# The second attention of a two-layer kernel: the probabilities turned by TensorE, or by VectorE in 32x32 blocks with DMAs that move the blocks

## The chip, the cores and the metric

One NeuronCore of a Trainium2 chip runs the whole program. The metric is the device time of one execution, in microseconds (us). The engines are TensorE (PE in the rows; PEld is its weight load), VectorE (DVE), ScalarE (ACT), GpSimd (POOL) and the sync engine (SP), which here only issues DMAs.

## The reference

Two layers over x of shape (16, 128, 128) and a context of (16, 128, 96), all float32: attention, a mixture of experts, attention, a routed expert network, each added to x. What is changed lies in the second attention, which for each of the 16 batches computes:

```
q_in = x @ Wq + lora                     # 128 tokens, 16 heads of 64
k_in, v_in = first 124 context rows @ Wk, Wv (+ lora)
out = softmax(q k^T / 8) v               # over 124 keys
out_ipa = softmax(q ki^T / 8) vi         # over the last 4 context rows
out = out + out_ipa
x = x + out @ Wo + bo + lora
```

The kernel keeps both softmaxes of a head side by side: 124 + 4 = 128 probabilities for each query. So a batch has a p1 of 128 queries x 16 heads x 128 keys, 1 MB in float32, and the product with the values needs it with the keys on the partitions.

## The kernel before

Each engine has one in-order program written by hand, with semaphores between them. The second attention is a loop of rounds, b = -1 to 16. In round b an engine works on the scores and the softmax of batch b, on the queries, keys and values of batch f = b + 1, on the outputs of batch t = b - 1, and on the first layer's experts of batch g = b + 4 (while g < 16). Z.name are the semaphores of this attention; `after(engine, sem, count)` is a wait that is left out where the count is zero or less.

TensorE's order in round b is: scores(b,0), turn(t,0), queries(f,0), turn(t,1), queries(f,1), ffn(g,0), scores(b,1), turn(t,2), keys(f,0), turn(t,3), ffn(g,1), outputs(t,0), outputs(t,1), keys(f,1), values(f,0), inputs(b+2), values(f,1), and the projection of batch t. A turn is 4 transposes of 128x128 (one head each) through an identity into a PSUM bank; VectorE's turned(t,n) copies the bank to p1T (in the last two batches ScalarE copies two of the four).

VectorE's shifted(b,n) takes the maxima from the scores of 4 heads, ScalarE's powers(b,n) makes the exponentials, VectorE's summed(b,n) the reciprocals, and GpSimd's norm(b,n) (L498) multiplies them in. ipa_norm(b) (L794 to L798) finishes the 4 extra keys of all 16 heads, so a turn needs it too (Z.ipa_p). VectorE ends its round with dve_residual(t), which waits for the projection, and with the statistics and the normalized input of later batches.

SP issues in round f one small DMA (L391, the extra values of batch f), and expert weights: 3 DMAs of 128 KB in rounds 2 to 7, 6 in rounds 13 to 15.

After round 16 comes the routed network, which starts when all outputs of the attention are copied (`pe.wait_ge(Z.o_sb, 2 * B)`).

Of the kernel before, what the change touches and what calls it, by code (L numbers as in the profile page):

```python
# [51 lines left out]
def build_program(nc, T, out):  # L52

    with ExitStack() as ctx:
# [29 lines left out]
        class Arena:  # L84
# [9 lines left out]
            def take(self, shape, dt=F32):  # L94
# [8 lines left out]
                if dt != F32:  # L103
# [151 lines left out]
        Z = named(sem, "z", "xn xb tr xT q q_sb k0 k1 k0_sb k1_sb ki v v_sb vi0 vi1 score ipa_max maxed ipa_exp ipa_step ipa_p "  # L255
                            "exp rsum norm turned p_sb p_odd o o_sb proj x_new stats")

# [13 lines left out]
        FILL = 2  # L271
        LAST_TURNS = B - 2
        SPARE = 14
# [14 lines left out]

        def p_copied(t, n):

            done = CH * min(t, LAST_TURNS) + 2 * max(t - LAST_TURNS, 0) + n + 1
            if t < LAST_TURNS:
                return Z.p_sb, done
            return (Z.p_odd, 2 * (t - LAST_TURNS) + n // 2 + 1) if n % 2 else (Z.p_sb, done - n // 2)

# [61 lines left out]
        def _(sp):  # L357
# [51 lines left out]
        def _(pool):  # L409
# [84 lines left out]
            def norm(b, n):  # L494

                pool.wait_ge(Z.rsum, CH * b + n + 1)
                part = p1[:, b % 2, n, :, 0:ORG]
                pool.tensor_tensor(part, part, rsum1[:, b % 2, CH * n:CH * n + CH].unsqueeze(2).broadcast_to((128, CH, ORG)),  # L498
                                   ALU.mult).then_inc(Z.norm, 1)
# [64 lines left out]
        def _(dve):  # L564
# [226 lines left out]
            def ipa_norm(b):  # L791

                dve.wait_ge(Z.ipa_exp, b + 1)
                dve.tensor_reduce(ipa_sum[:, b % 2, :], ipa_s[:, b % 2, :, :], X, ALU.add).then_inc(Z.ipa_step, 1)  # L794
                dve.wait_ge(Z.ipa_step, b * 2 + 1)
                dve.reciprocal(ipa_sum[:, b % 2, :], ipa_sum[:, b % 2, :]).then_inc(Z.ipa_step, 1)
                dve.wait_ge(Z.ipa_step, b * 2 + 2)
                dve.tensor_tensor(p1[:, b % 2, :, :, ORG:S].rearrange("p n c j -> p (n c) j"), ipa_s[:, b % 2, :, :],  # L798
                                  ipa_sum[:, b % 2, :].unsqueeze(2).broadcast_to((128, H, IPA)), ALU.mult)\
                    .then_inc(Z.ipa_p, 1)  # L800
# [74 lines left out]
            def round1(b):  # L875
                f, t, g = b + 1, b - 1, b + 4
                if there(b):
                    shifted(b, 0)
                if there(t):
                    turned(t, 0)  # L880
# [4 lines left out]
                if there(t):  # L885
                    turned(t, 1)
                if b == 15:
# [19 lines left out]
                if b == 12:  # L907
                    hidden(0)
                if there(t):
                    turned(t, 2)  # L910
                if b == 15:
# [9 lines left out]
                if there(t):  # L921
                    turned(t, 3)
                if b == 13:
# [131 lines left out]
        def _(act):  # L1055
# [89 lines left out]
            def powers(b, n):  # L1145

                act.wait_ge(Z.maxed, CH * b + n + 1)
                for c in range(CH):
                    h = CH * n + c
                    ins = act.activation(p1[:, b % 2, n, c, 0:ORG], blocks(bank[n])[:, c, 0:ORG], ACT.Exp,  # L1150
                                         bias=negmax1[:, b % 2, h:h + 1], accum_out=sums1[:, b % 2, h:h + 1])
# [18 lines left out]
            def turned(t, n):  # L1170

                act.wait_ge(Z.turned, CH * t + n + 1)
                act.activation(p1T[:, CH * n:CH * n + CH, :], blocks(bank[(4, 6, 5, 4)[n]]), ACT.Copy).then_inc(Z.p_odd, 1)

# [28 lines left out]
            def round1(b):  # L1203
# [11 lines left out]
                if there(b):  # L1215
                    powers(b, 1)
                if b == 15:
                    turned(t, 1)
                if there(f):
# [11 lines left out]
                if b == 15:  # L1231
                    turned(t, 3)
                    gathered(1)
                if b == B:
                    gathered(4)
                    turned(t, 1)
                    gathered(5)
                    turned(t, 3)
                if there(b):
# [88 lines left out]
        def _(pe):  # L1328
# [185 lines left out]

            def turn(t, n, freed, count):

                pe.wait_ge(Z.norm, CH * t + n + 1)
                pe.wait_ge(Z.ipa_p, t + 1)
                after(pe, freed, count)
                for c in range(CH):  # L1520
                    mm = pe.transpose(blocks(bank[(4, 6, 5, 4)[n]])[:, c, :], p1[:, t % 2, n, c, :], ident[:, :])  # L1521
                mm.then_inc(Z.turned, 1)

            def queries(f, n, freed, count):
# [16 lines left out]
            def outputs(t, n, freed, count):  # L1541

                for k in (2 * n, 2 * n + 1):
                    pe.wait_ge(*p_copied(t, k))
                pe.wait_ge(Z.v_sb, 2 * t + n + 1)
                pe.wait_ge((Z.vi0, Z.vi1)[t % 2], 16 * (t // 2 + 1))
                after(pe, freed, count)
                for c in range(CH):
                    for odd in range(2):
                        h = 8 * n + 2 * c + odd  # L1550
                        mm = pe.matmul(blocks(bank[5 - n])[D1 * odd:D1 * odd + D1, c, :], v1[:, t % 2, D1 * h:D1 * h + D1],  # L1551
                                       p1T[:, CH * (2 * n + odd) + c, :], start=True, stop=True)
                mm.then_inc(Z.o, 1)
# [58 lines left out]
            def round1(b):  # L1612
# [4 lines left out]
                if there(b):  # L1617
                    scores(b, 0)
                if there(t):
                    turn(t, 0, Z.o_sb, 2 * t)  # L1620
                if b == B:
# [11 lines left out]
                if there(f):  # L1633
                    queries(f, 0, Z.v_sb, 2 * f - 1)
                if there(t):
                    if b == B:
                        pe.wait_ge(G.xg, 4)
                    turn(t, 1, Z.v_sb, 2 * min(f, B))
                if b == B:
# [4 lines left out]
                if there(f):  # L1644
                    queries(f, 1, *((Z.p_sb, CH * t + 1) if there(t) else (Z.q_sb, 2 * f)))
                if b == 12:
# [5 lines left out]
                if there(b):  # L1652
                    scores(b, 1)
                if there(t):
                    turn(t, 2, *((Z.q_sb, 2 * f + 1) if there(f) else (Z.v_sb, 2 * B - 1)))
                if b == B:
                    gather(5)
                if b == 15:
                    gather(0)
                    tell(1, *p_copied(t, 1))  # L1660
                if there(f):
                    keys(f, 0, *((Z.p_sb, CH * t + 2) if there(t) else (Z.v_sb, 2 * f)))
                if b == -1:
                    pe.wait_ge(W.added, QUERIES_ADDED)
                    fold(6)
                if there(t):
                    turn(t, 3, *((Z.q_sb, 2 * f + 2) if there(f) else p_copied(t, 0)))
                if b == 13:
# [7 lines left out]
                if there(t):  # L1676
                    outputs(t, 0, *p_copied(t, 2))
                if b == 15:
# [4 lines left out]
                if there(t):  # L1683
                    outputs(t, 1, *p_copied(t, 3))
                if b == 12:
# [193 lines left out]
```

## Time and profile before

| what | us |
|---|---|
| time, median of 3 runs (lowest, highest) | 517.43 (515.69, 517.9) |
| span of the profiled execution, first to last instruction | 513.1 |
| busy: PE / PEld / DVE / ACT / POOL | 487.3 / 378.7 / 354.2 / 288.2 / 234.4 |
| second attention: first scores(0,0) to the start of outputs(15,1) | 135.16 to 389.06 |
| mean granted clock of TensorE | 0.989 |

The profile holds the span of its execution, and no time of its own around it; the median of the timed runs is 4.3 us above the span. Busy time is the sum in which an engine executes; for PE the ends of matmuls are modelled.

### The profile page before, as it was taken

How to read it: one execution, taken by the hardware profiler on the slowest of the kernel's cores; microseconds unless marked ns; L12 is line 12 of the kernel's file. 1: busy time of each engine (PE TensorE's matmuls, PEld its weight loads, DVE VectorE, ACT ScalarE, POOL GpSimd, SP SyncE). 2: the span in 40 equal slices, each digit the busy share in tenths (PEclk: the TensorE clock that was granted, in tenths of full speed). 3: DMA queues.
4: the chain of work that ended last, by engine and by line, in shares of the span. 5: the costliest groups of instructions: out<-in, count | busy, mean ns of one | idle time of the engine just before them, and what ended most of it. 6: DMA issues, size and time to landing. Idle time of an engine off the chain costs nothing.

```text
span 513.1 us, 13570 instructions
## 1 busy us (share of the span) xinstructions
PE 487.3 (95%) x5109; PEld 378.7 (74%) x5113; DVE 354.2 (69%) x1000; ACT 288.2 (56%) x984; POOL 234.4 (46%) x331
## 2 busy tenths in 40 slices
PE   4799999998999999999999999899999999999996
PEld 3466766656668778887787777788757897799995
DVE  5888989766786678566786665757866588535553
ACT  3366566463586776666867657665664444413332
POOL 4845545035365544575444755324231980090440
PEclk9699999999999999999999999999999999999999
DMA  8900000000001100111000000022202100000001
GB/s 229 234 3 4 3 3 3 3 1 8 4 1 32 34 20 16 34 33 34 3 2 2 4 3 3 1 66 64 64 0 71 56 0 1 1 22 24 1 2 42
DMA packets 21872, 14.48 MB, mean 28 GB/s; under 512 B 5928, under 2 KB 21136, under 8 KB 21808
## 3 DMA queue, kind: packets, MB, share of 16 engines
q1 hardware_dynamic: 20704, 13.31, 9.6%
q8 instruction: 42, 0.69, 0.6%
q10 hardware_dynamic: 1104, 0.30, 0.3%
q14 instruction: 22, 0.18, 0.1%
HBM read 12.30 MB, written 1.05 MB: 26 GB/s over the span
## 4 chain that ended last, share of the span: by engine, by line
PE 79%; DVE 12%; ACT 3%; issue 2%; DMA 1%; POOL 1%; ACTq 0%; DVEq 0%; POOLq 0%
PE bank L1792 9%; PE bank L1721 6%; PE bank L1551 5%; PE bank L1558 5%; PE bank L1801 5%; PE bank L1538 5%; PE bank L1510 5%; PE bank L1374 5%; PE bank L1463 5%; PE bank L1521 4%; PE bank L1530 4%; PE bank L1808 3%; PE bank L1609 3%; PE bank L1359 3%; ACT work L1150 2%
## 5 line engine op out<-in xcount | busy, mean ns | idle before, releaser
L1150 ACT ACTIVATE work<-bank,negmax 128x124 f32<-128x124 f32 x256 | 90.0, 387 | 52.2 <-DVE ipa_s L775 52.0
L498 POOL TENSOR_TENSOR work<-work,rsum 128x496 f32<-128x496 f32 x64 | 64.1, 1012 | 120.2 <-DVE rsum L789 120.2
L533 POOL TENSOR_SCALAR work<-work,slot 128x128 f32<-128x128 f32 x64 | 49.7, 792 | 48.3 <-DVE slot L864 29.4
L1150 ACT ACTIVATION_READ_ACCUMULATOR work<-bank,negmax 128x1 f32 x256 | 58.9, 230 | 0.0
L1792 PE MATMUL bank<-work 128*128 128x256 f32 x224 | 53.4, 381 | 0.0
L1014 DVE SCALAR_TENSOR_TENSOR work<-work,bank 128x256 f32<-128x256 f32 x64 | 26.9, 421 | 33.0 <-ACT work L1302 32.8
L1302 ACT ACTIVATE work<-bank 128x256 f32<-128x256 f32 x64 | 24.5, 383 | 40.6 <-PE bank L1792 29.1
L481 POOL TENSOR_TENSOR work<-work 128x512 f32<-128x512 f32 (+2 forms) x48 | 39.2, 817 | 12.1 <-DVE work L745 9.6
L306 DVE TENSOR_TENSOR x_all<-bank,x_all 128x128 f32<-128x128 f32 x16 | 4.7, 292 | 57.4 <-PE bank L1721 55.4
L1792 PEld LDWEIGHTS bank<-work 128*128 128x128 f32 x224 | 40.3, 190 | 4.7 <-DVE work L1017 0.2
L773 DVE TENSOR_REDUCE negmax<-bank 128x4 f32<-128x496 f32 x64 | 42.5, 664 | 0.0
L432 POOL TENSOR_TENSOR rstd<-veps,minus_half 128x1 f32<-128x1 f32 (+3 forms) x28 | 21.2, 755 | 46.1 <-DVE veps L575 45.8
L783 DVE COPY work<-bank 128x512 f32<-128x512 f32 x60 | 40.9, 681 | 0.8 <-PE bank L1521 0.8
L1510 PEld LDWEIGHTS bank<-work 64*128 64x128 f32 x512 | 31.1, 187 | 13.9 <-ACT work L1157 7.6
L629 DVE TENSOR_REDUCE negmax<-bank 128x8 bf16<-128x1024 f32 x32 | 39.1, 1221 | 2.2 <-PE bank L1344 1.7
L1521 PE MATMUL bank<-ident,work 128*128 128x128 f32 x256 | 40.1, 279 | 0.1
L1510 PE MATMUL bank<-work 64*128 64x128 f32 x512 | 37.2, 285 | 1.1 <-issue 1.1
L1090 ACT ACTIVATE work<-bank 128x1024 f32<-128x1024 f32 x32 | 31.0, 1021 | 11.8 <-PE bank L1359 11.8
L1551 PEld LDWEIGHTS bank<-work 128*64 128x64 f32 x512 | 27.7, 136 | 13.5 <-issue 8.7
L1721 PEld LDWEIGHTS bank<-work 128*128 128x128 f32 x256 | 31.1, 192 | 7.4 <-ACT work L1163 5.4
L1530 PE MATMUL bank<-xT,work 128*128 128x128 f32 x256 | 34.3, 278 | 1.6 <-DVE work L783 1.4
L1538 PE MATMUL bank<-cT_all,work 96*128 96x124 f32 x256 | 35.1, 280 | 0.0
(197 smaller groups left out, 1101.1 us busy)
## 6 DMA issues: line engine op xcount, KB each, us to landing
work<-in_L_ffn_w_dram SPq DMA_DIRECT2D x42, 128.0 KB, 2.3
x_all<-in_x_dram SPq DMA_DIRECT2D x4, 256.0 KB, 5.8
out_dram<-x_all SPq DMA_DIRECT2D x4, 256.0 KB, 2.6
ctx_all<-in_ctx_dram SPq DMA_DIRECT2D x4, 192.0 KB, 6.0
ctx_all<-in_L_ffn_w_dram SPq DMA_DIRECT2D x6, 128.0 KB, 2.3
work<-in_L_xattn_Wq_dram SPq DMA_DIRECT2D x1, 512.0 KB, 6.5
work<-in_L_xattn_Wo_dram SPq DMA_DIRECT2D x1, 512.0 KB, 8.2
work<-in_L_ffn_We_dram SPq DMA_DIRECT2D x1, 512.0 KB, 5.7
```

The lines of the kernel that those rows point to most:

```text
L498: pool.tensor_tensor(part, part, rsum1[:, b % 2, CH * n:CH * n + CH].unsqueeze(2).broadcast_to((128, CH, ORG)), ALU.mult).then_inc(Z.norm, 1)
L533: ins = pool.tensor_scalar(ohw_of(e)[:, k, :], count[:, :], slot[:, h, 0, k, e % E1:e % E1 + 1], slot[:, h, 1, k, e % E1:e % E1 + 1], ALU. ...
L773: dve.tensor_reduce(negmax1[:, b % 2, part], got_s[:, :, 0:ORG], X, ALU.max, negate=True)
L783: dve.tensor_copy(p1T[:, CH * n:CH * n + CH, :], blocks(bank[(4, 6, 5, 4)[n]])).then_inc(Z.p_sb, 1)
L1150: ins = act.activation(p1[:, b % 2, n, c, 0:ORG], blocks(bank[n])[:, c, 0:ORG], ACT.Exp, bias=negmax1[:, b % 2, h:h + 1], accum_out=sums1[ ...
L1510: mm = pe.matmul(blocks(bank[2 * half + odd])[:, c, :], q1T[rows, b % 2, CH * half + c, :], k1T[rows, b % 2, CH * half + c, :], start=True ...
L1521: mm = pe.transpose(blocks(bank[(4, 6, 5, 4)[n]])[:, c, :], p1[:, t % 2, n, c, :], ident[:, :])
L1530: mm = pe.matmul(blocks(bank[5 - n])[:, c, :], wq1[:, part], xT[:, f % 2, :], start=True, stop=True)
L1538: mm = pe.matmul(bank[6][:, ORG * c:ORG * c + ORG], wk1[0:C, part], cT_all[:, f, 0:ORG], start=True, stop=True)
L1551: mm = pe.matmul(blocks(bank[5 - n])[D1 * odd:D1 * odd + D1, c, :], v1[:, t % 2, D1 * h:D1 * h + D1], p1T[:, CH * (2 * n + odd) + c, :], s ...
L1721: mm = pe.matmul(bank[7][:, 0:D], o1T[:, c, :], wo1[:, c, :], start=(c == 0), stop=(c == 7))
L1792: mm = pe.matmul(halves(bank[4 + c])[:, n, :], up_weights(e, n, c), xgT[e // E1][:, :, e % E1, :], start=True, stop=True)
```

## The change

TensorE turns nothing any more. VectorE's turned(b,n) now belongs to batch b itself, at the end of its round: one transpose instruction for 4 heads reads p1 (128 x 512) and writes p1B, in which each 32x32 block is turned but still lies on the partitions of its queries. A half of a batch is 8 heads, that is 2 such instructions. SP's moves(b,half) then issues 16 DMAs, one for each pair of 32-partition groups (from i to j), each of 32 rows of 1 KB, so that p1T gets the keys on the partitions. outputs(t,half) waits for all 16 (p_moved). p1 has one buffer in place of two; p1B and p1T have one for each half. moves(b,half) waits until outputs(b-1,half) has read p1T, and turned(b,n) until the moves of batch b-1 have read p1B.

```
@@ buffers
-        p1 = work.take([128, 2, CH, CH, S])
-        p1T = work.take([128, H, S])
+        p1 = work.take([128, CH, CH, S])
+        p1B = work.take([128, 2, 4, 8, 32])
+        p1T = work.take([128, 2, 4, 8, 32])
...
+        def p_moved(t, half):
+
+            return (Z.moved0, Z.moved1)[half], 16 * MOVES * (t + 1)
@@ SP
+            def moves(b, half):
+
+                sp.wait_ge(Z.turned, CH * b + 2 * half + 2)
+                after(sp, Z.o, 2 * (b - 1) + half + 1)
+                for i in range(4):
+                    for j in range(4):
+                        sp.dma_start(p1T[tile_rows(j), half, i, :, :], p1B[tile_rows(i), half, j, :, :])\
+                            .then_inc((Z.moved0, Z.moved1)[half], 16)
             for f in range(B):
...
+                moves(f, 0)
+                moves(f, 1)
@@ DVE
-            def turned(t, n):
-
-                if t >= LAST_TURNS and n % 2 == 1:
-                    return
-                dve.wait_ge(Z.turned, CH * t + n + 1)
-                dve.tensor_copy(p1T[:, CH * n:CH * n + CH, :], blocks(bank[(4, 6, 5, 4)[n]])).then_inc(Z.p_sb, 1)
+            def turned(b, n):
+
+                half, odd = n // 2, n % 2
+                dve.wait_ge(Z.norm, CH * b + n + 1)
+                dve.wait_ge(Z.ipa_p, b + 1)
+                if b > 0:
+                    dve.wait_ge(*p_moved(b - 1, half))
+                dve.transpose(p1B[:, half, :, CH * odd:CH * odd + CH, :].rearrange("p j c q -> p c j q"),
+                              p1[:, n, :, :].rearrange("p c (j k) -> p c j k", j=4)).then_inc(Z.turned, 1)
...
                     ipa_norm(b)
+                    for n in range(CH):
+                        turned(b, n)
@@ PE
-            def turn(t, n, freed, count):
...
             def outputs(t, n, freed, count):
 
-                for k in (2 * n, 2 * n + 1):
-                    pe.wait_ge(*p_copied(t, k))
+                pe.wait_ge(*p_moved(t, n))
...
-                                       p1T[:, CH * (2 * n + odd) + c, :], start=True, stop=True)
+                                       p1T[:, n, :, CH * odd + c, :], start=True, stop=True)
```

The order of TensorE in one middle round, before. L1510 is scores, L1521 turn, L1530 queries, L1538 keys, L1463 ffn, L1551 outputs:

```order
L1510 MATMUL bank<-work 128x128 x8
L1521 MATMUL bank<-ident,work 128x128 x4
L1530 MATMUL bank<-xT,work 128x128 x4
L1521 MATMUL bank<-ident,work 128x128 x4
L1530 MATMUL bank<-xT,work 128x128 x4
L1463 MATMUL bank<-work 128x512
L1510 MATMUL bank<-work 128x128 x8
L1521 MATMUL bank<-ident,work 128x128 x4
L1538 MATMUL bank<-cT_all,work 128x124 x4
L1521 MATMUL bank<-ident,work 128x128 x4
L1463 MATMUL bank<-work 128x512
L1551 MATMUL bank<-work 64x128 x16
```

And the same round in the changed kernel, where L1505 is scores, L1516 queries, L1524 keys, L1458 ffn, L1536 outputs:

```order
L1505 MATMUL bank<-work 128x128 x8
L1516 MATMUL bank<-xT,work 128x128 x8
L1458 MATMUL bank<-work 128x512
L1505 MATMUL bank<-work 128x128 x8
L1524 MATMUL bank<-cT_all,work 128x124 x4
L1458 MATMUL bank<-work 128x512
L1536 MATMUL bank<-work 64x128 x16
```

The four turns are gone, and the rest keeps its order. The end of a round on VectorE in the changed kernel, from the second softmax (L805 to L809) over the transposes (L793) to the residual (L304) and the next round's maxima (L780), with the semaphores that each waits for:

```order
L805 TENSOR_REDUCE ipa_sum<-ipa_s 128x16 [waits z_ipa_exp]
L807 RECIPROCAL ipa_sum<-ipa_sum 128x16 [waits z_ipa_step]
L809 TENSOR_TENSOR work<-ipa_s,ipa_sum 128x16x4 [waits z_ipa_step]
L793 STREAM_TRANSPOSE work<-work 128x4x4x32 [waits z_moved0,z_ipa_p,z_norm] x2
L793 STREAM_TRANSPOSE work<-work 128x4x4x32 [waits z_moved1,z_ipa_p,z_norm] x2
L304 TENSOR_TENSOR x_all<-bank,x_all 128x128 [waits z_xb,z_proj]
```

Before, the row of L798 was followed at once by the residual, and the copies out of the turns stood between the maxima. SP's queue in one of the rounds 3 to 7 of the changed kernel, where L397 is the small DMA of the values, L383 and L384 the expert weights, and L392 the moves:

```order
L397 DMA work<-work 4x1024 [waits z_o,w_taken]
L383 DMA work<-in_L_ffn_w_dram 128x256 x2
L384 DMA work<-in_L_ffn_w_dram 128x2x128
L392 DMA work<-work 32x256 [waits z_o,z_turned]
L392 DMA work<-work 32x256 x15
L392 DMA work<-work 32x256 [waits z_o,z_turned]
L392 DMA work<-work 32x256 x15
```

Before, the rows of L392 weren't there. They are 32 DMAs for each of the 16 batches.

## Rows read from the trace of the kernel before

**Rows 1.** The page's busy times, with the share of the span and instructions.

```profile
PE 487.3 (95%) x5109; PEld 378.7 (74%) x5113; DVE 354.2 (69%) x1000; ACT 288.2 (56%) x984; POOL 234.4 (46%) x331
```

**Rows 2.** Windows, one whole round: length, busy time (count), clock, DMA share.

```profile
241.81:257.41 15.60, 15.44 (x138) 12.17 (x137) 11.04 (x34) 10.71 (x45) 7.92 (x12) 1.00 0.01 3
```

**Rows 3.** Timeline of PE in that round: start, length, line, shapes, count.

```profile
241.81 1.16 PE L1510 MATMUL bank<-work 64*128 64x128 f32 x16
242.90 0.66 PE L1521 MATMUL bank<-ident,work 128*128 128x128 f32 x4
243.39 1.06 PE L1530 MATMUL bank<-xT,work 128*128 128x128 f32 x8
244.28 0.60 PE L1521 MATMUL bank<-ident,work 128*128 128x128 f32 x4
244.72 1.06 PE L1530 MATMUL bank<-xT,work 128*128 128x128 f32 x8
...
246.57 1.16 PE L1510 MATMUL bank<-work 64*128 64x128 f32 x16
...
251.69 1.09 PE L1551 MATMUL bank<-work 128*64 128x128 f32 x16 [0.16 <-DVE work L783]
...
257.41 1.16 PE L1510 MATMUL bank<-work 64*128 64x128 f32 x16
```

**Rows 4.** Timeline of DVE in that round.

```profile
243.75 0.68 DVE L783 COPY work<-bank 128x512 f32<-128x512 f32 x1
244.35 0.17 DVE L772 TENSOR_REDUCE ipa_max<-bank 128x4 f32<-128x16 f32 x1
...
252.78 0.62 DVE L798 TENSOR_TENSOR work<-ipa_s,ipa_sum 128x64 f32<-128x64 f32 x1
257.52 0.29 DVE L306 TENSOR_TENSOR x_all<-bank,x_all 128x128 f32<-128x128 f32 x1 [4.13 <-PE bank L1721]
```

**Rows 5.** Timeline of ACT in that round: the exponential of the extra keys.

```profile
251.78 0.29 ACT L1240 ACTIVATE ipa_s<-ipa_s 128x64 f32<-128x64 f32 x1
```

**Rows 6.** Timeline of SP's queue: start and length of DMA issues.

```profile
17.87 0.43 SPq L371 DMA_DIRECT2D work<-in_L_xattn_v_up_dram  x1
...
205.36 0.60 SPq L391 DMA_DIRECT2D work<-work  x1
206.00 0.92 SPq L385 DMA_DIRECT2D work<-in_L_ffn_w_dram  x2
206.96 0.43 SPq L386 DMA_DIRECT2D work<-in_L_ffn_w_dram  x1
```

**Rows 7.** DMAs by issue: KB each, median us from issue to landing.

```profile
work<-in_L_ffn_w_dram SPq DMA_DIRECT2D x42, 128.0 KB, 2.3
...
work<-in_L_ffn_router_w_dram SPq DMA_DIRECT2D x1, 64.0 KB, 1.8
```

**Rows 8.** DMA queue from 200 to 300 us: packets, MB, share of 16 engines.

```profile
q1 hardware_dynamic: 1728, 1.28, 4.5%
```

**Rows 9.** Windows near the start, columns as in rows 2 (PE's busy time second).

```profile
15.00:16.00 1.00, 0.00 (x0) 0.00 (x0) 1.00 (x1) 0.79 (x4) 1.00 (x2) 1.00 1.11 221
18.00:19.00 1.00, 1.00 (x6) 0.44 (x5) 0.97 (x7) 0.36 (x2) 1.00 (x3) 0.50 0.80 175
```

**Rows 10.** Timeline of PE there: one transpose at the high and one at the low clock.

```profile
17.07 0.28 PE L1402 MATMUL bank<-ident,xn_in 128*128 128x128 f32 x1
...
26.61 0.47 PE L1402 MATMUL bank<-ident,xn_in 128*128 128x128 f32 x1
```

**Rows 11.** Timeline of PE: scores(0,0), scores(1,0), scores(1,1), and outputs(15,1).

```profile
135.16 1.16 PE L1510 MATMUL bank<-work 64*128 64x128 f32 x16 [1.06 <-issue]
...
146.56 1.16 PE L1510 MATMUL bank<-work 64*128 64x128 f32 x16
152.89 1.16 PE L1510 MATMUL bank<-work 64*128 64x128 f32 x16
...
389.06 1.09 PE L1551 MATMUL bank<-work 128*64 128x128 f32 x16
```

More of the change, by code:

```diff
@@ L255, in build_program @@
         Z = named(sem, "z", "xn xb tr xT q q_sb k0 k1 k0_sb k1_sb ki v v_sb vi0 vi1 score ipa_max maxed ipa_exp ipa_step ipa_p "
-                            "exp rsum norm turned p_sb p_odd o o_sb proj x_new stats")
+                            "exp rsum norm turned moved0 moved1 o o_sb proj x_new stats")
         R = named(sem, "r", "wide count tok picks xn tr xT hid th h logit max ex step topx top turned slot")
@@ L271, in build_program @@
         FILL = 2
-        LAST_TURNS = B - 2
+        MOVES = 16
         SPARE = 14
@@ L496, in norm @@
                 pool.wait_ge(Z.rsum, CH * b + n + 1)
-                part = p1[:, b % 2, n, :, 0:ORG]
+                part = p1[:, n, :, 0:ORG]
                 pool.tensor_tensor(part, part, rsum1[:, b % 2, CH * n:CH * n + CH].unsqueeze(2).broadcast_to((128, CH, ORG)),
@@ L797, in ipa_norm @@
                 dve.wait_ge(Z.ipa_step, b * 2 + 2)
[L798 removed]
+                dve.tensor_tensor(p1[:, :, :, ORG:S].rearrange("p n c j -> p (n c) j"), ipa_s[:, b % 2, :, :],
                                   ipa_sum[:, b % 2, :].unsqueeze(2).broadcast_to((128, H, IPA)), ALU.mult)\
@@ L878, in round1 @@
                     shifted(b, 0)
-                if there(t):
-                    turned(t, 0)
                 if b == B:
@@ L884, in round1 @@
                     shifted(b, 1)
-                if there(t):
-                    turned(t, 1)
                 if b == 15:
@@ L908, in round1 @@
                     hidden(0)
-                if there(t):
-                    turned(t, 2)
                 if b == 15:
@@ L920, in round1 @@
                         .then_inc(Z.k0_sb, 1)
-                if there(t):
-                    turned(t, 3)
                 if b == 13:
@@ L1149, in powers @@
                     h = CH * n + c
-                    ins = act.activation(p1[:, b % 2, n, c, 0:ORG], blocks(bank[n])[:, c, 0:ORG], ACT.Exp,
+                    ins = act.activation(p1[:, n, c, 0:ORG], blocks(bank[n])[:, c, 0:ORG], ACT.Exp,
                                          bias=negmax1[:, b % 2, h:h + 1], accum_out=sums1[:, b % 2, h:h + 1])
@@ L1168, in values @@
                 act.activation(v1[0:ORG, f % 2, 512 * n:512 * n + 512], bank[5 + n][0:ORG, :], ACT.Copy).then_inc(Z.v_sb, 1)
-            def turned(t, n):
-                act.wait_ge(Z.turned, CH * t + n + 1)
-                act.activation(p1T[:, CH * n:CH * n + CH, :], blocks(bank[(4, 6, 5, 4)[n]]), ACT.Copy).then_inc(Z.p_odd, 1)
             def inputs(b):
@@ L1216, in round1 @@
                     powers(b, 1)
-                if b == 15:
-                    turned(t, 1)
                 if there(f):
@@ L1231, in round1 @@
                 if b == 15:
-                    turned(t, 3)
                     gathered(1)
@@ L1235, in round1 @@
                     gathered(4)
-                    turned(t, 1)
                     gathered(5)
-                    turned(t, 3)
                 if there(b):
@@ L1513, in scores @@
                             mm.then_inc(Z.score, 1)
-            def turn(t, n, freed, count):
[L1517 to L1522, printed above, removed]
             def queries(f, n, freed, count):
@@ L1618, in round1 @@
                     scores(b, 0)
-                if there(t):
-                    turn(t, 0, Z.o_sb, 2 * t)
                 if b == B:
@@ L1634, in round1 @@
                     queries(f, 0, Z.v_sb, 2 * f - 1)
[L1635 to L1638, printed above, removed]
                 if b == B:
@@ L1644, in round1 @@
                 if there(f):
-                    queries(f, 1, *((Z.p_sb, CH * t + 1) if there(t) else (Z.q_sb, 2 * f)))
+                    queries(f, 1, *((Z.o_sb, 2 * t) if there(t - 1) else (Z.q_sb, 2 * f)))
                 if b == 12:
@@ L1653, in round1 @@
                     scores(b, 1)
-                if there(t):
-                    turn(t, 2, *((Z.q_sb, 2 * f + 1) if there(f) else (Z.v_sb, 2 * B - 1)))
                 if b == B:
@@ L1659, in round1 @@
                     gather(0)
-                    tell(1, *p_copied(t, 1))
+                    tell(1, Z.v_sb, 2 * B)
                 if there(f):
-                    keys(f, 0, *((Z.p_sb, CH * t + 2) if there(t) else (Z.v_sb, 2 * f)))
+                    keys(f, 0, Z.v_sb, 2 * f)
                 if b == -1:
@@ L1665, in round1 @@
                     fold(6)
-                if there(t):
-                    turn(t, 3, *((Z.q_sb, 2 * f + 2) if there(f) else p_copied(t, 0)))
                 if b == 13:
@@ L1676, in round1 @@
                 if there(t):
-                    outputs(t, 0, *p_copied(t, 2))
+                    outputs(t, 0, *((Z.q_sb, 2 * f + 1) if there(f) else (Z.v_sb, 2 * B - 1) if b < B else (Z.o_sb, 2 * t - 1)))
                 if b == 15:
@@ L1683, in round1 @@
                 if there(t):
-                    outputs(t, 1, *p_copied(t, 3))
+                    outputs(t, 1, *((Z.q_sb, 2 * f + 2) if there(f) else (Z.o_sb, 2 * t)))
                 if b == 12:
```

5 lines of the change are left out of this document (removed).

## The prediction, made before the changed kernel ran

> **What bounds the kernel now.** I read the page's busy times first: TensorE is busy for 95% of the span [rows 1]. A share over the whole span is no proof for one stage, so I cut out one round of the second attention: in 15.60 us PE is busy 15.44, while VectorE has 11.04, ScalarE 10.71 and GpSimd 7.92 [rows 2]. The round is TensorE's own work, back to back. VectorE's timeline shows where the slack lies: its last softmax step starts at 252.78 and it then stands 4.13 us until the projection is there [rows 4]. SP issues a few DMAs in a round and waits otherwise. I name times in a round from its start, S (scores(b,0), 241.81 in [rows 3]).
>
> **What goes from TensorE.** A turn costs the distance to the next group: 243.39 - 242.90 = 0.49, and 244.72 - 244.28 = 0.44; four in a round are 1.86 us [rows 3]. In 16 batches that is 29.8 us, and all of it lies on the path of today. A regular round would shrink from 15.6 to 13.7.
>
> **What moves on VectorE.** It loses a copy of a bank, pitch 244.35 - 243.75 = 0.60 us, four times in a round, and gets four block transposes of the same 128x512 elements. The trace has no such instruction. Its nearest row is that copy, so I take 0.60. As bounds: half of it, 0.30, and, with the second softmax's step of 0.62 for 64 elements as a sign that patterns with short runs can cost far more per element, three times it, 1.8 [rows 4]. VectorE's sum stays equal. The place changes: a transpose needs norm and the second softmax of its own batch. ScalarE's exponential for it starts at S + 9.97 [rows 5], VectorE's three steps end with the one at S + 10.97 + 0.62 = S + 11.6. Without the copies VectorE is there some 2.4 us earlier, but ScalarE is not, which saves about 0.4. So ipa_norm ends at S + 11.2, and two transposes later, at S + 12.4, the first half is ready; the second at S + 13.6. The norms are not late: GpSimd is busy for half of the round [rows 2], and the last norm needs only exp(b,3), before the row of [rows 5]. All this fits into the 4.13 us in which VectorE stood, so the transposes themselves I cost at nothing. That cover is gone if they take over 1 us each.
>
> **What comes on SP.** This is the term that decides. The issues of 128 KB in [rows 6] have a pitch of 0.48 us (206.00 to 206.96 for two), and 0.43 is the length of one; L371 has 32 rows, like a move, and also 0.43. So I take 0.475 us for one move, 7.6 us for the 16 of a half, 15.2 for a batch. That alone is as long as today's round. The only DMA of today from SBUF to SBUF, L391 with 4 rows, takes 0.60, pitch 0.64 [rows 6]: upper bound, 20.5 us for a batch. As a lower bound I take 0.43 without a gap: 13.8. For the landing I have 1.8 us for 64 KB and 2.3 for 128 KB from the issue [rows 7]; a move is 32 KB, I take 2.0 from the start of the last issue, which is 1.6 after its end (bounds 1.4 and 1.9). The bytes themselves are cheap: 4.5% of 16 engines over 100 us for 1728 packets is 42 ns each [rows 8]; 512 packets of a half are 21.5 us on one engine, 1.3 us on 16, and run beside the issues.
>
> The Trainium skill's page "DMA: Bandwidth & Descriptors", section "Why a DMA increments its semaphore by 16 and not by 1", says that a copy uses the largest number of engines up to 16 that divides its outer dimension, and that the sequencer itself writes the rest of the 16 counts. By that the 4-row L391 pays for 12 writes and a 32-row move pays for none, so it speaks for 0.475 and not for 0.64; the sum by the one is 575, by the other 632 (both below). No row here shows a 32-row copy within SBUF.
>
> **The new path.** Let E be the end of the issues of moves(b,1).
> - outputs(b,1) starts at E + 1.6.
> - From outputs(t,1) to the next round's scores TensorE needs 257.41 - 251.69 = 5.7 us (keys, values, projection) [rows 3], so S(b+2) = E + 7.3. What VectorE and ScalarE do there fits in as before.
> - The first half of batch b+2 is turned at S + 12.4, and with 0.1 for the hand-over SP begins moves(b+2,0) at E + 19.8.
> - 15.2 us later moves(b+2,1) is issued.
> This is a cycle of 35.0 us in two rounds, 17.5 a round, with SP waiting some 1.7 us in a round. SP's own queue gives nearly as much: 15.2 + 0.64 for L391, and 3 x 0.475 more in rounds 2 to 7, that is 17.3 there. The second half lands last, and TensorE waits for it: a round has 13.7 us of its work, so it stands some 3.8 us, in front of outputs(t,1).
>
> **The sum.** From the start of scores(0,0): first half of batch 0 turned at 12.5, its 32 moves and those of batch 1 with one L391 behind them 15.2 + 0.6 + 15.2, landing 1.6, so outputs(1,1) starts at 45.1. Seven cycles of two rounds to outputs(15,1): 245. Together 290.1. Before, this stretch was 389.06 - 135.16 = 253.9 [rows 11]. The difference is +36.2. Some rounds have more of their own between the scores and the softmax: in round 1 the two scores are 152.89 - 146.56 = 6.3 apart against 4.8 in a regular one (scores(b,1) at 246.57) [rows 3, 11]; such work (round 5, the routing of rounds 12 to 15, 6 weight DMAs in front of the moves of 13 to 15) now lies on the path. I allow 6 us. That makes +42.2, span 555.3, and with the 4.3 us between the span and the median 559.6.
>
> **The clock.** The one stretch of this trace with gaps on PE shows what they do: PE idles through 15 to 16 us, and in 18 to 19 the granted clock is 0.50, the level of 1.2 GHz [rows 9]. The same transpose takes 0.28 us at 17.07 and 0.47 at 26.61, so the low level lasts for several us of work [rows 10]. In the changed kernel PE stands nearly 4 us in each round, and right behind the gap come the 5.7 us that lie on the cycle. Lower bound: nothing, if the clock holds. Upper bound: all 5.7 at the low level, longer by 5.7 x (0.47/0.28 - 1) = 3.9 for each cycle, and some 2 more where the scores behind them are late, 5.9 x 7.5 = 44 us. I take 2 us for each cycle, 15 in all: the clock falls in most rounds but is back within them. This gives 559.6 + 15 = 575.
>
> **The rivals.**
> 1. *An SBUF to SBUF move costs as L391 does, 0.64.* SP is then never idle: 12.5 + 16 x 20.5 + 15 x 0.64 + 36 weight DMAs x 0.475 + 1.6 = 369 against 253.9, +115, 632; the clock does not add, as TensorE no longer sets the pace. For it: the same kind of copy in the same queue. Against it: its 4 rows, while those of 32 and of 128 rows lie at 0.43. Chance 0.09.
> 2. *The moves hide, and TensorE's 29.8 us come out.* The mechanism would be that issues overlap or cost far less than 0.43. With the cycle above at two regular rounds of today (30.8) 32 issues may take 11.0, 0.34 each; below this the change pays. All would give 517.4 - 29.8 = 488; as ScalarE's copies then come close to setting the round, 495 is more like it. No row of [rows 6] has under 0.43. Chance 0.04. The Trainium skill's same page, section "Issuing engines are not separate DMA queues", says that the time to initiate a DMA "is usually small relative to the DMA itself"; by that this rival would hold. Here the issue is 0.43 us, and the 32 packets of a move on 16 engines are some 0.1 us [rows 6, 8], so the trace speaks against it.
> 3. *The transposes are dear.* At 1.8 us each, the first half is ready 2.4 us later, 18 us over 7.5 cycles, and VectorE's 13 us of other and new work still fit into 17.5. It gives 593, inside the range, and has no chance of its own.
> 4. *The new waits just use up what TensorE saves*: a cycle of 30 to 31 us, 515 to 520. Chance 0.02.
> 5. *Slower, but by under 25 us*, because more of SP's issues and of the tail overlap than I see (0.43, landing 1.4, transposes at 0.30): cycle 35.0 - 1.4 - 0.2 - 0.6 = 32.8, -17 us, and no fall of the clock: 543. With a little less extra work it is below my range: chance 0.05.
>
> **Range and chances.** My own case, the cycle through SP at 0.475, has 0.80. Its range goes from 542 (rival 5's values nearly all at once) to 612 (the clock at its upper bound gives 604, and transposes somewhat over 0.60 the rest). This leaves out rival 1 with 0.09, rival 5 with 0.05, and the faster and equal ones with 0.06. The range 542 to 612 stands for all cases. Within 0.5% (2.6 us, about what a measurement of this kernel tells from no change) I put 0.02, faster 0.04, slower 0.94.
>
> **What would show it.** In the changed profile: SP's queue has rows of some 7.5 us for 16 moves and is issuing for 85% or more of a round; PE idles before L1536, put down to a DMA; rounds (L1505 to L1505) are 17.5 to 19 us; VectorE's transposes are near 0.6; PEclk has digits below 9 in the slices of the attention; PE's busy time is 30 us less, if the clock holds. The prediction is wrong if a move issues in under 0.35 or over 0.55 us, if the landing takes over 3 us, or if the clock falls and stays low for whole rounds.

## The result and the profile after

| | before | changed |
|---|---|---|
| time, median of 4 runs | 516.83 us (515.69 to 517.9) | 645.49 us (643.56 to 647.62) |
| ratio to before | 1 | 1.2498 (95%: 1.246 to 1.2535) |
| span of the profiled execution | 513.1 us | 641.8 us |
| mean granted clock of TensorE | 0.989 | 0.874 |

The sign was forecast, the size was not: 645 lies outside 542 to 612 and near the 632 of the first rival. The page of the changed kernel, beside [rows 1]: busy times with shares, the granted clock in 40 slices, the chain that ended last by engine, and two groups (busy time and mean ns, then the idle time before them):

```profile
PE 514.1 (80%) x4853; PEld 386.6 (60%) x4857; DVE 359.4 (56%) x1004; ACT 287.2 (45%) x980; POOL 233.9 (36%) x331
...
PEclk9699999989597688879679777986886679999999
...
SPq 47%; PE 36%; DVE 6%; issue 6%; DMA 3%; ACT 2%; POOL 0%; DVEq 0%; POOLq 0%
...
L1536 PE MATMUL bank<-work 128*64 128x128 f32 x512 | 49.7, 356 | 92.7 <-DMA work<-work 92.7
```

Almost half of the chain is SP's queue, that is, the issuing itself and not the data on its way (DMA 3%). TensorE has 256 instructions fewer and is yet busy for 27 us longer, because its clock falls. In front of the outputs it stands 92.7 us. Now SP's timeline over two rounds, beside [rows 6]:

```profile
285.44 20.79 SPq L392 DMA_DIRECT2D work<-work  x32
306.32 0.62 SPq L397 DMA_DIRECT2D work<-work  x1
306.99 0.91 SPq L383 DMA_DIRECT2D ctx_all<-in_L_ffn_w_dram  x2
307.94 0.43 SPq L384 DMA_DIRECT2D ctx_all<-in_L_ffn_w_dram  x1
308.47 20.92 SPq L392 DMA_DIRECT2D work<-work  x32
```

The 32 moves of a batch take 20.8 us, 0.65 each, and behind them come at once the small DMA, the weights and the next batch's moves: in these two rounds SP doesn't wait at all. All moves by their source line, with length (min/median/max, ns) and landing, and VectorE's transposes in the same view:

```profile
L392 SPq DMA_DIRECT2D work<-work x512: 512/591/2027, 147.5 to 513.3; - x171
...
DMA to landing us min/median/max: 1.8/1.8/3.5
```
```profile
L793 DVE STREAM_TRANSPOSE work<-work x64: 668/671/712, 146.2 to 492.0; 128x512 f32<-128x512 f32 x64
...
  DMA work<-work: 34.0, 15
```

A move is 0.59 long, and from its start to the next one's it is 0.633 (medians; I call this the pitch); the landing is 1.8 where 2.0 was taken; a transpose is 0.67 (pitch 0.63) where 0.60 was taken. What TensorE sees of it, one round as in [rows 3], with the idle time in brackets:

```profile
292.15 1.16 PE L1505 MATMUL bank<-work 64*128 64x128 f32 x16
...
299.14 1.13 PE L1458 MATMUL bank<-work 128*128 128x512 f32 x2 [0.81 <-ACT work L1116]
300.20 1.09 PE L1536 MATMUL bank<-work 128*64 128x128 f32 x16
307.55 1.97 PE L1536 MATMUL bank<-work 128*64 128x128 f32 x16 [6.26 <-DMA work<-work]
```

The two halves of the outputs are 7.35 us apart, and behind the gap the same 16 matmuls take 1.97 instead of 1.09: the level of 1.2 GHz. The windows of this round, the longest behind the first two, and of another one (columns as in [rows 2]):

```profile
292.20:317.30 25.10, 18.03 (x122) 13.21 (x122) 11.92 (x34) 10.81 (x45) 7.90 (x11) 0.80 0.23 63
224.90:246.60 21.70, 17.11 (x122) 12.64 (x121) 11.03 (x37) 10.71 (x45) 7.91 (x11) 0.84 0.23 65
```

**Where the time is.** From scores(0,0) at 133.83 to the last outputs at 515.18 it is 381.35 us, where [rows 11] give 253.9; this stretch holds 127.5 of the 129 us. SP issues moves from 147.5 to 513.9. Rival 1's sum has 369 for the stretch. Of the 512 moves, 15 take over 0.8 us and up to 2.03; what they take beyond 0.59 is 11.8 us together. With these the 12 us between 369 and 381 are accounted for; what else differs from the sum (a pitch of 0.633 for 0.64, a first move 1.2 us later, 2 to 3 us of waits on SP) nearly cancels.

The trace shows something beside each of the 15. The DMA queues from 147.5 to 514 us and from 452.6 to 454.7, the time of the longest issue (packets, MB, share of 16 engines):

```profile
q8 instruction: 15, 0.25, 0.3%
```
```profile
q8 instruction: 1, 0.02, 4.2%
```

So a second queue, which the profile calls `instruction`, has 15 packets of 16 KB in this stretch, and each of the 15 long issues overlaps one of them: the one of 2.03 us starts at 452.66, its packet runs from 452.90 to 454.32. No run changed only these packets, so this is a coincidence in time, 15 of 15, and not a shown cause.

### The profile page after: what moved, and what is told of

It is laid out like the page before. It is cut to its first block, busy times and chain, and to the rows that moved or that the text cites. A ratio compares the mean times of both kernels' runs of the same rounds, so it can differ in the third digit from the quotient of the medians.

```text
span 641.8 us, 13599 instructions
## 1 busy us (share of the span) xinstructions
PE 514.1 (80%) x4853; PEld 386.6 (60%) x4857; DVE 359.4 (56%) x1004; ACT 287.2 (45%) x980; POOL 233.9 (36%) x331
## 4 chain that ended last, share of the span: by engine, by line
SPq 47%; PE 36%; DVE 6%; issue 6%; DMA 3%; ACT 2%; POOL 0%; DVEq 0%; POOLq 0%
SPq L392 44%; PE bank L1767 8%; PE bank L1776 4%; PE bank L1369 4%; PE bank L1783 2%; DMA work<-work 2%; PE bank L1354 2%; PE bank L1458 2%; PE bank L1594 1%; DVE negmax L637 1%; PE bank L1381 1%; DVE work L793 1%; ACT work L1155 1%; DMA ctx_all<-in_ctx_dram 1%; PE bank L1516 1%
## 5 line engine op out<-in xcount | busy, mean ns | idle before, releaser
L1536 PE MATMUL bank<-work 128*64 128x128 f32 x512 | 49.7, 356 | 92.7 <-DMA work<-work 92.7
L1536 PEld LDWEIGHTS bank<-work 128*64 128x64 f32 x512 | 39.2, 181 | 109.3 <-DMA work<-work 100.5
L304 DVE TENSOR_TENSOR x_all<-bank,x_all 128x128 f32<-128x128 f32 x16 | 4.7, 292 | 117.9 <-PE bank L1696 111.2
L1155 ACT ACTIVATION_READ_ACCUMULATOR work<-bank,negmax 128x1 f32 x256 | 63.7, 249 | 0.0
L793 DVE STREAM_TRANSPOSE work<-work 128x512 f32<-128x512 f32 x64 | 41.6, 690 | 35.5 <-DMA work<-work 34.0
L1252 ACT ACTIVATE work<-bank 128x496 f32<-128x496 f32 x16 | 9.4, 585 | 101.2 <-PE bank L1524 101.2
L440 POOL TENSOR_TENSOR rstd<-veps,minus_half 128x1 f32<-128x1 f32 (+3 forms) x28 | 21.2, 755 | 87.2 <-DVE veps L583 87.1
L1524 PE MATMUL bank<-cT_all,work 96*128 96x124 f32 x256 | 48.1, 346 | 0.3 <-DVE work L924 0.3
L1543 PE MATMUL bank<-work,cT_all 96*124 96x512 f32 x64 | 47.8, 845 | 0.1
L1524 PEld LDWEIGHTS bank<-cT_all,work 96*128 96x128 f32 x256 | 41.5, 245 | 8.0 <-issue 5.0
L1767 PEld LDWEIGHTS bank<-work 128*128 128x128 f32 x224 | 40.3, 190 | 4.7 <-DVE work L1022 0.2
L1696 PEld LDWEIGHTS bank<-work 128*128 128x128 f32 x256 | 35.9, 215 | 11.7 <-issue 9.3
L1458 PE MATMUL bank<-work 128*128 128x512 f32 x64 | 34.4, 626 | 8.7 <-ACT work L1116 8.7
```

Of the source, the lines that this page charges most:

```text
L793: dve.transpose(p1B[:, half, :, CH * odd:CH * odd + CH, :].rearrange("p j c q -> p c j q"), p1[:, n, :, :].rearrange("p c (j k) -> p c j k ...
L1155: ins = act.activation(p1[:, n, c, 0:ORG], blocks(bank[n])[:, c, 0:ORG], ACT.Exp, bias=negmax1[:, b % 2, h:h + 1], accum_out=sums1[:, b % ...
L1458: pe.matmul(blocks(to), xT0[:, g % 8, :], we[:, 4 * half:4 * half + 4, :], start=True, stop=True)\
L1524: mm = pe.matmul(bank[6][:, ORG * c:ORG * c + ORG], wk1[0:C, part], cT_all[:, f, 0:ORG], start=True, stop=True)
L1543: pe.matmul(bank[5 + n][0:ORG, :], cT_all[:, f, 0:ORG], wv1[0:C, 512 * n:512 * n + 512], start=True, stop=True)\
L1767: mm = pe.matmul(halves(bank[4 + c])[:, n, :], up_weights(e, n, c), xgT[e // E1][:, :, e % E1, :], start=True, stop=True)
```

## The experiments

Two theories had to be told apart. **Price:** a move is dear because both its ends lie in SBUF, whatever its rows. **Rows, bytes or traffic:** 0.633 comes of the row count, of 32 such copies in a row, or of crossing partitions. A third question was what TensorE's falling clock costs. The diffs show the lines that matter; the increments `.then_inc(...)`, the count MOVES, the declarations and the code around are left out.

**e1_price** is the kernel before, with five groups of DMAs in rounds 8 to 12 whose data nobody uses; only ScalarE's later copies of the gathered tokens wait for their end. In outline:

```diff
+ if f == 8:   sp.dma_start(probe[tile_rows(j), i, :], wq1[tile_rows(i), 256 * j:256 * j + 256])             # x16
+ if f == 9:   sp.dma_start(probe[tile_rows(j), i, :], T["L1_ffn_w1"][i, 32 * j:32 * j + 32, :])             # x16
+ if f == 10:  sp.dma_start(probe[:, i, :], wq1[:, 256 * i:256 * i + 256])                                   # x4
+ if f == 11:  sp.dma_start(probe[tile_rows(j), i, 0:64], wq1[tile_rows(i), 64 * j:64 * j + 64])             # x16
+ if f == 12:  sp.dma_start(probe[64 rows, i, 128 elements], wq1[64 rows, 128 elements])                     # x16
```

> The kernel before, with groups of DMAs added on SP's queue that nothing waits for before round 15: 16 from SBUF to SBUF with 32 rows of 1 KB; 16 from DRAM to SBUF with 32 rows of 1 KB; 4 from SBUF to SBUF with 128 rows of 1 KB; 16 from SBUF to SBUF with 32 rows of 256 bytes; 16 from SBUF to SBUF with 64 rows of 512 bytes. Theory (a source in SBUF makes the issue itself dearer, 0.59 us against 0.43, whatever the rows and bytes): pitch 0.63, 0.48, 0.64, 0.63, 0.63 us. Rival (any 16 small DMAs back to back are issued at 0.63): the DRAM group is at 0.63 too. Rival (bytes or the DMA engines set the pace): 256 bytes are cheaper than 1 KB, and 128 rows of 1 KB cost up to four times 32 rows. By all of them the time stays near 517, as nothing waits for SP there.

One run, 514.01 us, beside 516.68 (514.84 to 520.05) of the kernel before: issues that nothing waits for cost nothing. SP's timeline:

```profile
252.67 10.92 SPq L402 DMA_DIRECT2D work<-work  x16
...
267.94 7.41 SPq L404 DMA_DIRECT2D work<-in_L_ffn_w_dram  x16
...
283.16 2.47 SPq L406 DMA_DIRECT2D work<-work  x4
...
298.79 10.51 SPq L408 DMA_DIRECT2D work<-work  x16
...
315.07 10.93 SPq L410 DMA_DIRECT2D work<-work  x16
```

Within SBUF a copy has a pitch of 0.63 to 0.64 us for 32, 64 and 128 rows and for rows of 256 B to 1 KB; the same 32 rows of 1 KB out of DRAM (L404) 0.464. These are medians: in each group of 10.5 to 10.9 us one of the 16 issues took 1.03 to 1.42. The second number is the prediction's 0.475. It was the price of another kind of copy.

**e10_sides** asked in the same way which side matters: SBUF to DRAM; SBUF to SBUF on the same 32 partitions; DRAM to DRAM; and within SBUF 16 rows and 4 rows, 16 DMAs each. In outline:

```diff
+ if f == 8:   scratch[rows]      <- wq1[32 rows, 256]         # SBUF -> DRAM
+ if f == 9:   probe[32 rows]     <- wq1[the same 32 rows]     # SBUF -> SBUF
+ if f == 10:  scratch[32 rows]   <- L1_ffn_w1[32 rows]        # DRAM -> DRAM
+ if f == 11:  probe[16 rows]     <- wq1[16 rows]              # SBUF -> SBUF
+ if f == 12:  probe[4 rows]      <- wq1[4 rows]               # SBUF -> SBUF
```

> The kernel before, with five groups of 16 DMAs that nothing waits for before round 15: from SBUF to DRAM, 32 rows of 1 KB; within SBUF and within the same 32 partitions, 32 rows; from DRAM to DRAM, 32 KB; within SBUF, 16 rows; within SBUF, 4 rows. Theory (the issue is dear only where both sides lie in SBUF): pitches 0.48, 0.63, 0.48, 0.63, and 0.63 to 0.65 for 4 rows. Rival (a source in SBUF is enough): the first group is at 0.63 too. Rival (the crossing of partitions makes it dear): the second group is at 0.48. Rival (fewer than 16 rows add 0.17 us, as the prediction read L391): the 4-row group is some 0.17 above the 16-row one, 0.80. The time stays near 515.

One run, 514.49 us, beside one of the kernel before with 513.82:

```profile
253.16 7.70 SPq L403 DMA_DIRECT2D scratch_dram<-work  x16
...
268.43 10.82 SPq L405 DMA_DIRECT2D work<-work  x16
...
283.66 10.49 SPq L407 DMA_DIRECT2D scratch_dram<-in_L_ffn_w_dram  x16
...
299.28 10.48 SPq L409 DMA_DIRECT2D work<-work  x16
...
315.54 9.90 SPq L411 DMA_DIRECT2D work<-work  x16
```

The pitches are 0.464, 0.633, 0.632, 0.632 and 0.620 (medians; the second to the fourth group have one long issue each, of 0.97 to 1.36). The third was expected at 0.48 and missed: DRAM to DRAM is as dear as SBUF to SBUF. So in these rows it is not SBUF as source or target that makes a copy dear, nor the crossing of partitions, but both sides in the same memory. Four rows are no dearer than 32.

**e2_rows64** leaves the changed kernel as it is, but moves the same bytes in 8 DMAs of 64 rows for each half (the blocks land in wrong partitions).

```diff
-                for i in range(4):
+                for i in range(2):
                     for j in range(4):
-                        sp.dma_start(p1T[tile_rows(j), half, i, :, :], p1B[tile_rows(i), half, j, :, :])
+                        rows = slice(64 * i, 64 * i + 64)
+                        sp.dma_start(p1T[rows, half, j, :, :], p1B[rows, half, j, :, :])
```

> The changed kernel with 8 moves of 64 rows in a half in place of 16 of 32 rows: the same bytes and the same buffers, but blocks land on other partitions than the computation needs. Theory (SP's count of issues sets the pace, 0.63 us each): SP needs 10.1 us for a batch, the cycle of two rounds is 5.7 + 12.5 + 10.1 + 1.6 = 30 us, 15 a round, and the time 510 to 525 (with some low clock up to 535). Rival (bytes or packets set it): 1 MB for a batch is moved as before, and the time stays near 645.

It took 531.65 us (528.52 to 533.04), ratio 1.0267 (1.0203 to 1.033), within what was allowed if the clock falls (its mean is 0.959). SP's timeline:

```profile
242.93 10.07 SPq L393 DMA_DIRECT2D work<-work  x16
```

The price of each is nearly the same, a pitch of 0.64; there are half as many, and 114 us of the 129 are gone. So neither the bytes nor the traffic made the time.

**e3_one** moves a half with one DMA of 128 rows of 4 KB (wrong partitions again): the change with its queue nearly free.

```diff
+                sp.dma_start(p1T[:, half, :, :, :], p1B[:, half, :, :, :])
```

> The changed kernel with one move of 128 rows of 4 KB for each half: again the same bytes, wrong partitions. Theory (only SP's issues make the change slow): the rest of the change shows its gain, rounds of 13.7 to 14.5 us set by TensorE and ScalarE, 490 to 500. Rival (VectorE's transposes at the round's end, the single p1 and the waits cost as well): 510 or more.

It took 508.7 us (507.66 to 509.42), ratio 0.9836 (0.9782 to 0.989): 1.6% faster, but 490 to 500 was expected. Each of its moves is issued behind a wait and is 0.47 us long. TensorE's timeline has a wait in front of the second ffn group of each round that was not there before:

```profile
250.03 1.12 PE L1455 MATMUL bank<-work 128*128 128x512 f32 x2 [0.82 <-ACT work L1113]
```

Rounds are 14.7 us against 15.6: of the 1.86 taken from TensorE, 0.9 come back as waiting for ScalarE, and round 1 takes 20.3 where it took 16.8. So even free moves bring 8 us and not the 29.8 or 22 of rival 2.

**e4_split** issues 8 of the 32 moves from ScalarE's queue, at the end of its round.

```diff
-                for i in range(4):
+                for i in range(4 if half == 0 else 2):
@@ ACT, behind values(f, 1)
+                    act.wait_ge(Z.turned, CH * b + 4)
+                    after(act, Z.o, 2 * b)
+                    for i in (2, 3):
+                        for j in range(4):
+                            act.dma_start(p1T[tile_rows(j), 1, i, :, :], p1B[tile_rows(i), 1, j, :, :])
```

> The changed kernel with the last 8 of a batch's 32 moves issued by ScalarE at the end of its round; all blocks go where they must. Theory (SP's queue sets 22.6 us a round at 0.63 a move): SP has 24 x 0.63 = 15.2 us for a batch, the very number that I had predicted for 32, and ScalarE's 8 x 0.6 fit into its idle time; the cycle is 35 us for two rounds and the time 555 to 580, the clock's share included. Rival (the DMA engines or the transfers set the pace, not the issuing engine): it stays above 630.

It took 594.03 us (592.25 to 595.77), ratio 1.1485 (1.1415 to 1.1554); 555 to 580 was expected. ScalarE's timeline, then TensorE's:

```profile
251.51 6.06 ACTq L1273 DMA_DIRECT2D work<-work  x8
257.62 0.36 ACT L1155 ACTIVATE work<-bank,negmax 128x124 f32<-128x124 f32 x1 [6.46 <-issue]
```
```profile
262.55 2.08 PE L1465 MATMUL bank<-work 128*128 128x512 f32 x2 [4.13 <-ACT work L1116]
```

Eight fewer issues on SP give 51 us, but on ScalarE they are 6 us in front of the next round's exponentials (median pitch 0.64; in this group two long ones, of 1.37 and 0.87 us, make it 0.76 on average), and TensorE waits for ScalarE, here for its product of the expert outputs (L1116). The price is the issuing engine's, whichever of the two it is.

**e6_twelve** makes the sum of the prediction true: 12 moves for each half (4 of 64 rows, 8 of 32; some blocks land in wrong partitions), so 24 x 0.633 = 15.2 us a batch.

```diff
+                for j in range(4):
+                    rows = slice(64 * (j // 2), 64 * (j // 2) + 64)
+                    sp.dma_start(p1T[rows, half, j % 2, :, :], p1B[rows, half, j % 2, :, :])
-                for i in range(4):
+                for i in (2, 3):
```

> The changed kernel with 12 moves in a half (4 of 64 rows and 8 of 32; all bytes and buffers, some blocks on the wrong partitions), so that SP needs 24 x 0.633 = 15.2 us for a batch, the number that the prediction had put in for 32. Theory (only the price of an issue was wrong in the prediction, its cycle, its landing and its clock term hold): rounds of 17.5 us and a bit, time 560 to 590, with 575 as the sum had it. Rival (the cycle was wrong as well, and the issues at 0.63 hide that): outside of 555 to 595.

It took 582.25 us (579.8 to 584.4), ratio 1.1309 (1.1267 to 1.1351). Hit: the prediction's 575 for exactly this queue, its range 560 to 590. TensorE's timeline shows the cycle of two rounds, one half almost in time and the next late and at the low clock:

```profile
258.36 1.09 PE L1540 MATMUL bank<-work 128*64 128x128 f32 x16 [0.53 <-DMA work<-work]
...
264.09 1.16 PE L1509 MATMUL bank<-work 64*128 64x128 f32 x16
...
278.15 1.98 PE L1540 MATMUL bank<-work 128*64 128x128 f32 x16 [4.91 <-DMA work<-work]
...
285.48 1.16 PE L1509 MATMUL bank<-work 64*128 64x128 f32 x16
```

Rounds alternate, 15.5 and 21.0, 17.1 and 21.2, 15.4 and 21.4: pairs of 36.5 to 38.3, and 38.4 to 38.8 later on, where the cycle has 35.0 and 2 for the clock. From outputs(t,1) to the next scores (L1509) it is 5.7 us behind the short gap and 7.3 behind the long one: the low clock costs 1.6 in this cycle.

**e7_fill** and **e8_twelve_fill** put 24 transposes of the identity into the bank that outputs(t,n) is to overwrite, while TensorE would wait (before both halves in e7, before the second in e8; nobody reads them). e7 is otherwise the changed kernel, e8 is e6.

```diff
+                after(pe, freed, count)
+                for k in range((24, 24)[n]):           # e8: (0, 24)
+                    pe.transpose(blocks(bank[5 - n])[:, k % 4, :], ident[:, :], ident[:, :])
                 pe.wait_ge(*p_moved(t, n))
...
-                after(pe, freed, count)
```

> The changed kernel with 24 more transposes of the identity on TensorE in front of each outputs(t,n), written to the bank that the outputs overwrite: 2.8 us of work in each of its two gaps of a round, which lifts the granted clock. Theory (SP's queue alone sets the rounds, the low clock costs nothing): clock above 0.93, time within 1% of the changed kernel's 645. Rival (the clock takes 15 us or more, as the prediction had it): 630 or less.

> The kernel with 12 moves in a half and 24 such transposes in front of outputs(t,1) alone. There the cycle runs through TensorE's stretch behind the gap. If the low clock costs the 1 to 2 us for each cycle of the prediction, this kernel is 7 to 15 us faster than the same without the filler, unless the filler's 2.8 us are longer than the gap. Rival (the clock costs nothing there either): the same time or slower.

e7: 645.38 us (641.9 to 646.88), ratio 1.2513 (1.2451 to 1.2575), the time of the changed kernel. e8: 570.85 us (569.09 to 573.87), ratio 1.1074 (1.1017 to 1.1132), 11.4 less than e6. Their granted clocks in 40 slices, e7 and then e8, to be read against the row above:

```profile
PEclk9999999989799899799989999989968889999999
```
```profile
PEclk9999999998989999999999999999898999999999
```

The mean clock rises from 0.874 to 0.961 in e7 and from 0.944 to 0.984 in e8. One gains nothing, because SP sets the pace and TensorE only waits less long; the other gains 11 us, because there TensorE's tail lies on the cycle. The 11 are net of what 2.8 us of filler cost where the gap was shorter (0.53 us in the row above), so the low clock may cost e6 more than that.

e7 also bears on the long issues: with its 768 transposes more, the stretch of its moves has 21 packets of the `instruction` queue where the changed kernel has 15, and 20 long issues where that has 15, each beside such a packet.

**e5_dram** takes every block to where the change takes it, with fewer issues: a half of p1B is stored to DRAM in one DMA and comes back in four, one for each target tile of 32 rows.

```diff
+            def stored(b, half):
+                sp.wait_ge(Z.turned, CH * b + 2 * half + 2)
+                if b > 0:
+                    sp.wait_ge(*p_moved(b - 1, half))
+                sp.dma_start(scratch[half, :, :], p1B[:, half, :, :, :].rearrange("p j c q -> p (j c q)"))
             def moves(b, half):
+                sp.wait_ge((Z.wrote0, Z.wrote1)[half], 16 * (b + 1))
                 after(sp, Z.o, 2 * (b - 1) + half + 1)
+                for j in range(4):
+                    sp.dma_start(p1T[tile_rows(j), half, :, :, :].rearrange("p i c q -> p i (c q)"),
+                                 scratch[half, :, 256 * j:256 * j + 256].rearrange("(i k) x -> k i x", i=4))
@@ DVE, turned(b, n)
-                    dve.wait_ge(*p_moved(b - 1, half))
+                    dve.wait_ge((Z.wrote0, Z.wrote1)[half], 16 * b)
```

> The changed kernel with the moves through DRAM: for each half one store of the turned blocks (128 rows of 4 KB) and four loads (32 rows of four runs of 1 KB), 10 issues for a batch in place of 32, all blocks where they must be; VectorE waits only for the store. Theory (SP's issues were the cost, 0.63 for a copy within SBUF and about 0.48 for one with DRAM): SP needs 5 us for a batch, and the rounds are near those of the one-move kernel (14.7 us), time 505 to 516. Rival (a store and a load in a row are too slow: 2 x 2.5 us and the issues end after TensorE wants the outputs): a wait of some us in front of the outputs in every round, 525 to 560.

It took 511.52 us (507.87 to 515.31, 10 runs), ratio 0.9901 (0.9873 to 0.9929): 1% faster than before. SP's timeline and then the landings (KB each, median us from issue):

```profile
253.69 1.51 SPq L392 DMA_DIRECT2D scratch_dram<-work  x2
256.28 4.51 SPq L400 DMA_DIRECT2D work<-scratch_dram  x8
```
```profile
scratch_dram<-work SPq DMA_DIRECT2D x32, 512.0 KB, 2.6
...
work<-scratch_dram SPq DMA_DIRECT2D x128, 128.0 KB, 3.1
```

Ten issues instead of 32, of the cheap kind (0.33 us for a store, each behind a wait, and a pitch of 0.474 for the loads), and a trip of 2.6 + 3.1 us that fits into the round. A round is 14.7 us, as in e3.

**e9_dram_swap** is e5 with ffn(g,1) behind outputs(t,0), to cover the wait for ScalarE.

```diff
+                if there(t):
+                    outputs(t, 0, ...)
                 if there(g):
                     pe.wait_ge(F.ys0, g + 1)
                     ffn(g, 1, bank[7])
-                if there(t):
-                    outputs(t, 0, ...)
```

> The kernel with the moves through DRAM, with ffn(g,1) behind outputs(t,0) on TensorE instead of in front of it. In the version without this TensorE waits 0.8 us in each middle round in front of ffn(g,1), for ScalarE's product of the expert outputs. Theory: outputs(t,0) fills that wait, 12 rounds by 0.8 to 1 us, 500 to 504. Rival (the loads from DRAM land later than outputs(t,0) would then like, or ScalarE's copies are the next limit): 507 or more.

It took 509.43 us (506.69 to 512.8), ratio 0.988 (0.9818 to 0.9943): the interval overlaps e5's, so no gain was shown, and 500 to 504 was missed. The wait for ScalarE is smaller, but the outputs come earlier and wait for the loads. Total waits for these (us, times, longest), e5 and then e9:

```profile
PEld bank L1547 <- DMA work<-scratch_dram: 7.5, 5, 3.2
```
```profile
PEld bank L1547 <- DMA work<-scratch_dram: 16.0, 15, 3.5
```

## Why the prediction was wrong, step by step

- **What comes on SP: the step that failed.** "So I take 0.475 us for one move." The rows behind it, L371 and the weights in [rows 6], are DMAs with DRAM on one side. The only row of the right kind was L391, 0.64, and it was set aside for its 4 rows. e1 and e10 show 0.62 to 0.64 for 4, 16, 32, 64 and 128 rows within SBUF, and 0.464 for 32 rows out of DRAM. The Trainium skill's page "DMA: Bandwidth & Descriptors", section "Why a DMA increments its semaphore by 16 and not by 1", has the sequencer do additional writes where a copy uses under 16 engines. The trace does not contradict that they are made, but no time for them is seen: 0.620 at 4 rows, 0.632 at 16.
- **What follows from it.** 0.16 us x 512 moves are 81 us. The cycle through TensorE (35.0 for two rounds) is then shorter than SP's own queue (some 42 to 46), the mechanism of rival 1, which had a chance of 0.09. Its 632 lacked the 11.8 us of long issues.
- **The sum itself.** With moves that take 15.2 us a batch, as assumed, it holds: e6 gives 582 against 575, in the pattern of two rounds. Long issues are in no term of it either.
- **What goes from TensorE.** The 1.86 us do leave the round, but e3 and e5 show that about half returns as a wait for ScalarE. Here this changes nothing; rival 2's 488 to 495 was too good by 14 us or more.
- **VectorE's transposes** are 0.67 us against 0.60, and wait rather than being waited for: right. **The landing** is 1.8 against 2.0: right.
- **The clock.** Gaps on PE pull it down, as said. The cost of 15 us, 2 a cycle, belongs to the cycle through TensorE, where e6 shows 1.6 in one cycle and e6 less e8 is 11. In the changed kernel it is nothing (e7), as rival 1 had it.
- **What would show it.** "The prediction is wrong if a move issues in [...] over 0.55 us": it does, 0.59. SP issuing for 85% of a round, the idle time before L1536, and the digits below 9 came as listed. Rounds of 17.5 to 19 did not: they are 20.7 to 25.1 after the first two, as SP's price says. The low clock did not stay for a whole round: the mean of a round is 0.74 to 0.92.

Not settled: how a packet of the `instruction` queue would lengthen an issue, which it does not always do (one of e10 falls into the group of 4 rows, at 318.47, and no issue there is over 0.60); and what makes a copy within one memory dearer. Neither was tried.

## What to carry to other kernels

Before data movement is taken off a compute engine and given to DMAs, count the issues for each queue in a round and multiply by the price of an issue of the same kind, with both ends in the same memories; that product, not the bytes, was 20.8 us against a round of 15.6. Here the one row of the right kind, of an odd shape, came nearer than several tidy rows of another kind. Fewer and larger DMAs, even by way of DRAM, turned 25% slower into 1% faster, and filling TensorE's gaps pays only where TensorE sets the pace.

## What the runs showed of the hardware

- Behind another of its kind, an issue on SP had a pitch of 0.464 us from DRAM to SBUF (e1) and from SBUF to DRAM (e10), and of 0.632 within DRAM (e10), each for 32 rows of 1 KB. Within SBUF it was 0.63 to 0.64 for 16 to 128 rows of 256 B to 1 KB, and 0.620 for 4 rows (e1, e2, e10). On ScalarE a move had 0.64 (e4).
- Behind a wait an issue was shorter: 0.53 us for a move (e4), 0.47 us for 128 rows of 4 KB within SBUF (e3), 0.33 for the same from SBUF to DRAM (e5), where in a row it is 0.59 and 0.42 for 32 rows of 1 KB.
- 15 of 512 issues in the changed kernel were long, 0.91 to 2.03 us, and each overlapped a packet of 16 KB in the queue that the profile calls `instruction`; in e7 20 of 20.
- Behind a gap of 6.26 us TensorE ran 16 matmuls in 1.97 us at 1.2 GHz (granted clock 0.50 from 307.6 to 309.4), where the half in front of the gap took 1.09 at 2.4 GHz (1.00 from 299.1 to 301.2). With filler in the gaps and the same total time, the mean clock was 0.961 instead of 0.874 (e7).
